# The fourth block's scores and attention moved behind the experts, and a later turn of the first expert's tokens

## The reference

```python
y = xn @ U                                   # 128 -> 32
dist = n[:, None] + n[None, :] - 2 * y @ y.T # n = sum(y*y), per block
attn = softmax(-dist) @ xn                   # 512 x 512 per block

probs = softmax(rms(xn) @ router_w.T)        # 8 experts, the best 2
dispatch = the first 320 tokens of each expert, in order
routed += w * ((silu(xg @ rg[e]) * (xg @ ru[e])) @ rd[e])   # inner size 512
shared = (silu(xn @ sg) * (xn @ su)) @ sd                   # inner size 1024
out = x + attn + shared + routed
```

## Time and profile before

| | us |
|---|---|
| median of 3 runs | 157.55 (156.96 to 157.59) |
| the profiled execution, its own time | 156.88 |
| its span, first to last instruction | 155.4 |
| PE busy | 150.5 |
| DVE busy | 117.4 |
| ACT busy | 103.5 |
| POOL busy | 83.2 |

### The profile page before, as it was taken

The page is one execution under the profiler, slowest core; times in us unless marked ns, Lnnn a source line. Parts: engine busy times, 40 slices in busy tenths (PEclk is TensorE's granted clock), DMA queues, the critical chain, the costliest instruction groups (busy, mean ns, idle before and its releaser), DMA issues.

```text
span 155.4 us, 3117 instructions
## 1 busy us (share of the span) xinstructions
PE 150.5 (97%) x964; PEld 135.1 (87%) x964; DVE 117.4 (76%) x290; ACT 103.5 (67%) x217; POOL 83.2 (54%) x102
## 2 busy tenths in 40 slices
PE   6999999999999999999999999999999999999992
PEld 6878777889999888888888899999999999878991
DVE  3999969899735599998988777786786786546871
ACT  3369999999469397768756569889677466334100
POOL 7653422357777787877400005698988847454000
PEclk9999999999999999999999999999999999999999
DMA  4999999981111117435069300423232011118486
GB/s 128 302 275 111 210 308 343 343 245 54 55 53 51 51 54 218 158 80 172 0 173 259 124 0 2 152 58 98 67 103 72 25 46 34 30 32 291 96 273 186
DMA packets 26638, 20.72 MB, mean 133 GB/s; under 512 B 2333, under 2 KB 22840, under 8 KB 26624
## 3 DMA queue, kind: packets, MB, share of 16 engines
q1 hardware_dynamic: 24544, 17.76, 42.4%
q0 software_dynamic: 1792, 2.65, 5.6%
q10 hardware_dynamic: 288, 0.14, 0.3%
HBM read 12.36 MB, written 7.92 MB: 131 GB/s over the span
## 4 chain that ended last, share of the span: by engine, by line
PE 92%; DVE 2%; DMA 2%; ACT 1%; POOL 1%; issue 1%; DVEq 0%
PE bank L1259 9%; PE bank L1344 9%; PE bank L1179 8%; PE bank L1181 8%; PE bank L1180 8%; PE bank L1290 8%; PE bank L1284 8%; PE bank L1287 8%; PE bank L1400 5%; PE bank L1402 5%; PE bank L1401 5%; PE bank L1416 2%; PE bank L1244 2%; PE bank L1427 2%; DMA acc<-in_L_attn_x_dram 2%; PE bank L1199 1%
## 5 line engine op out<-in xcount | busy, mean ns | idle before, releaser
L673 ACT ACTIVATE silu<-bank 128x512 f32<-128x512 f32 (+1 forms) x64 | 33.3, 520 | 29.5 <-PE bank L1290 28.9
L567 POOL DMA_INDIRECT slots_dram<-row,slot_i x32 | 34.0, 1063 | 10.9 <-issue 9.4
L1010 DVE TENSOR_TENSOR bank<-bank,silu 128x320 f32<-128x320 f32 (+1 forms) x48 | 27.1, 565 | 15.5 <-ACT silu L673 12.6
L586 POOL DMA_INDIRECT routed_dram<-eo,xg x24 | 23.0, 957 | 11.5 <-DVE eo L1050 6.3
L1016 DVE TENSOR_TENSOR hid_lo<-bank,hid_hi 128x320 fp32r<-128x320 f32 (+1 forms) x48 | 26.2, 546 | 0.0
L681 ACT CAST hid_hi<-bank 128x320 fp32r<-128x320 f32 (+1 forms) x48 | 22.9, 477 | 0.0
L574 POOL TENSOR_TENSOR ew_lo<-sw_raw,ew_hi 128x1024 fp32r<-128x1024 f32 x3 | 7.2, 2414 | 19.3 <-ACT ew_hi L697 19.3
L1010 DVE TENSOR_TENSOR hid_s<-bank,silu 128x512 f32<-128x512 f32 x16 | 11.0, 686 | 5.6 <-PE bank L1181 5.2
L1344 PEld LDWEIGHTS bank<-sd,hid_s 128*128 128x128 f32 x128 | 14.8, 192 | 0.3
L1259 PEld LDWEIGHTS bank<-row,probs 128*128 128x128 f32 x128 | 14.8, 191 | 0.2
L1344 PE MATMUL bank<-sd,hid_s 128*128 128x128 f32 x128 | 15.0, 275 | 0.0
(11 more groups left out here) (204 smaller groups left out, 362.6 us busy)
## 6 DMA issues: line engine op xcount, KB each, us to landing
sw_raw<-in_L_ffn_rg_dram SPq DMA_DIRECT2D x8, 256.0 KB, 3.1
sw_raw<-in_L_ffn_ru_dram SPq DMA_DIRECT2D x8, 256.0 KB, 3.6
rd_raw<-in_L_ffn_rd_dram SPq DMA_DIRECT2D x8, 256.0 KB, 3.4
routed_dram<-fill SPq DMA_DIRECT2D x1, 2048.0 KB, 11.7
routed<-routed_dram SPq DMA_DIRECT2D x8, 256.0 KB, 4.1
slots_dram<-fill SPq DMA_DIRECT2D x1, 1300.0 KB, 12.2
xg<-slots_dram SPq DMA_DIRECT2D x8, 130.0 KB, 2.4
row<-row SPq DMA_DIRECT2D x1, 1024.0 KB, 7.7
```

Source lines behind the costliest of these rows:

```text
L567: G.indirect_dma_start(slots_dram, bass.IndirectOffsetOnAxis(slot_i[:, k, t:t + 1], 0), row[:, t, 0:RW], None, bounds_check=E * CAP - 1, o ...
L673: C.activation(silu[:, q % 2, 0:n], gate_bank(q)[:, 0:n], ACT.Silu).then_inc(silu_ready, 1)
L1010: V.tensor_tensor(hid, up[:, 0:n], silu[:, q % 2, 0:n], ALU.mult).then_inc(hid_ready, 1)
```

## The change

The scores and the attention of the fourth block leave the place before block 1. The scores now stand between the gate and up products of the last chunk of all, into other banks; the exponentials come at the end of ACT's program, into memory of the loaded weights; the two halves of attention stand inside `down_end_block`, between the second and the third group of the f32 down products. DVE adds the attention there, and SP's last two stores wait for it. The first expert's tokens are turned behind the last up product of block 2 and not behind its sixth chunk, and the down product that stood at the first expert's first chunk moves one step forward. The second pair of expert down weights gets another place (that of `xnT` of block 0), since the fourth block's `yL` and `yR` stay in use.

```diff
     def down_step(q):
+        if q == at["block", EARLY - 1, CS - 3]:
+            return at["block", EARLY - 1, CS - 1]
         return CLOSE if q == END else min(q + LAG, END + 1)
...
+        rd_hi, rd_lo = [[in_y[:, CS * D:CS * D + CR * D].rearrange("p (c d) -> p c d", c=CR),
+                         in_x[:, 0:CR * D].rearrange("p (c d) -> p c d", c=CR)]
+                        for in_y, in_x in ((yL, xnT_hi), (yR, xnT_lo))]
+        end_probs = sw_raw[:, :, :].rearrange("p s (j i) -> p (s j) i", i=S)
+        def probs_of(b):
+            return end_probs if b == B - 1 else probs[:, b % 2, :, :]
...
+        end_score_b = [bank[7], bank[4], bank[5], bank[6]]
+        end_down_b = [bank[0], bank[1]]
+        end_att_b = [bank[2], bank[3]]
...
             for h in range(2):
+                sp.wait_ge(att_added, 2 * (B - 1) + h + 1)
                 sp.wait_ge(block_added, B + h)
...
-                    if j == 0 and b >= 2:
+                    if j == 0 and b == B - 1:
+                        act.wait_ge(ew_split_pool, E - DVE_WEIGHTS)
+                    elif j == 0 and b >= 2:
                         act.wait_ge(att_done, 2 * (b - 1))
...
             def round_down_weights(e):
                 act.wait_ge(rd_loaded[e % 2], 16 * (e // 2 + 1))
+                if e == 1:
+                    act.wait_ge(chunk_done, CS)
...
             act.wait_ge(sd_loaded, 16)
-            exps(3)
             C.copy(sd_hi, sd[:, :, :]).then_inc(sd_hi_s, 1)
...
-                    elif c == 6:
+                    elif c == 7:
                         slots_hi(0)
...
+            exps(B - 1)
...
-            for b in range(1, B):
+            for b in range(1, B - 1):
                 add_attention(b, 0)
                 add_attention(b, 1)
...
-                    elif c == 6:
+                    elif c == 7:
                         slots_lo(0)
...
             end_block_sum(0)
+            dve.wait_ge(block_added, B)
+            add_attention(B - 1, 0)
+            add_attention(B - 1, 1)
+            dve.wait_ge(att_added, 2 * B)
             end_block_sum(1)
...
+                elif b == B - 1:
+                    pe.wait_ge(eo_ready, E)
+                    pe.wait_ge(hid_ready, len(ORDER) - 2)
+                    pe.wait_ge(xg_ready, E)
+                    pe.wait_ge(out_copied, len(JOBS))
...
             def down_end_block():
                 b = B - 1
-                first, second = turn_b[0], sums_b
-                pe.wait_ge(xg_ready, E)
-                pe.wait_ge(hid_ready, at["block", b, CS - 2])
+                first, second = end_down_b
+                pe.wait_ge(silu_ready, at["block", b, CS - 1])
+                pe.wait_ge(hid_ready, at["block", b, CS - 1])
                 down_tile(first[:, 0:D], 0, range(CS - 2))
-                pe.wait_ge(out_copied, len(JOBS))
                 down_tile(second[:, 0:D], 2, range(CS - 2))
                 pe.wait_ge(hid_ready, at["block", b, CS - 1] + 1)
                 down_tile(first[:, 0:D], 0, range(CS - 2, CS))
                 down_tile(first[:, D:2 * D], 1).then_inc(end_down, 1)
+                attend(b, 0)
+                attend(b, 1)
                 down_tile(second[:, 0:D], 2, range(CS - 2, CS))
                 down_tile(second[:, D:2 * D], 3).then_inc(end_down, 1)
...
             attend(2, 0)
-            scores(3)
             attend(2, 1)
-            attend(3, 0)
-            attend(3, 1)
...
+                    elif q == len(ORDER) - 1:
+                        between = lambda: scores(B - 1)
...
+                if (kind, i, c) == ("block", EARLY - 1, CS - 1):
+                    turn_slots(0)
                 for p in chunks_down(q):
                     down_chunk(p)
...
-                if (kind, i, c) == ("block", EARLY - 1, 5):
-                    turn_slots(0)
-                elif kind == "expert" and c == 0 and i + 1 < E:
+                if kind == "expert" and c == 0 and i + 1 < E:
                     turn_slots(i + 1)
```

More of the change, by code:

```diff
@@ L216, in down_weights_of @@
             if s < 2:
-                return rd_hi[:, s, :, :], rd_lo[:, s, :, :]
+                return rd_hi[s], rd_lo[s]
             return rd_more[:, s - 2, 0, :, :], rd_more[:, s - 2, 1, :, :]
@@ L228, in moe_attention_kernel @@
         assert CS == 2 * TG and B % 2 == 0
-        assert CS * D + 2 * CR * D <= T
+        assert CS * D + CR * D <= (B - 1) * S and CR * D <= S
         sd_hi, sd_lo = [t[:, 0:CS * D].rearrange("p (c d) -> p c d", c=CS) for t in (yL, yR)]
-        rd_hi, rd_lo = [t[:, CS * D:CS * D + 2 * CR * D].rearrange("p (s c d) -> p s c d", s=2, c=CR)
-                        for t in (yL, yR)]
+        rd_hi, rd_lo = [[in_y[:, CS * D:CS * D + CR * D].rearrange("p (c d) -> p c d", c=CR),
[4 more added lines that the diff above has]
+            return end_probs if b == B - 1 else probs[:, b % 2, :, :]
         turned_out = sb("turned_out", [P, S])
@@ L257, in moe_attention_kernel, with score_bank, att_bank @@
         turn_b = [bank[6], bank[7]]
+        end_score_b = [bank[7], bank[4], bank[5], bank[6]]
+        end_down_b = [bank[0], bank[1]]
+        end_att_b = [bank[2], bank[3]]
+        def score_bank(b, j):
+            return end_score_b[j] if b == B - 1 else bank[j]
+        def att_bank(b, h):
+            return end_att_b[h] if b == B - 1 else down_b[h]
         tokens_b = [bank[6], bank[0], bank[3], bank[0]]
@@ L662, in exps @@
                     act.wait_ge(score_done, t + 1)
-                    if j == 0 and b >= 2:
+                    if j == 0 and b == B - 1:
+                        act.wait_ge(ew_split_pool, E - DVE_WEIGHTS)
+                    elif j == 0 and b >= 2:
                         act.wait_ge(att_done, 2 * (b - 1))
-                    C.activation(probs[:, b % 2, j, :], bank[j][:, :], ACT.Exp, scale=2.0
+                    C.activation(probs_of(b)[:, j, :], score_bank(b, j)[:, :], ACT.Exp, scale=2.0
                                  ).then_inc(prob_ready, 1)
@@ L695, in round_weights @@
                     elif e >= 3:
-                        act.wait_ge(att_done, 2 * B)
+                        act.wait_ge(att_done, 2 * (B - 1))
                 C.copy(weights_of(e)[0][:, w, :], ew_raw[:, e % 2, w, :]).then_inc(ew_hi_s, 1)
@@ L994, in add_attention @@
                 dve.wait_ge(att_done, 2 * b + h + 1)
[L995 removed]
+                o = att_bank(b, h)[:, 0:2 * (D + 1)].rearrange("p (r c) -> p r c", r=2)
                 t = TG * b + 2 * h
@@ L1057, in end_block_sum @@
                 a = acc[:, t:t + 2, :].rearrange("p t d -> p (t d)")
-                V.tensor_tensor(a, (turn_b[0], sums_b)[h][:, 0:2 * D], a, ALU.add).then_inc(block_added, 1)
+                V.tensor_tensor(a, end_down_b[h][:, 0:2 * D], a, ALU.add).then_inc(block_added, 1)
             def add_routed(k, g):
@@ L1116, in _ @@
             add_attention(0, 1)
-            for b in range(1, B):
+            for b in range(1, B - 1):
                 add_attention(b, 0)
                 add_attention(b, 1)
-                if b == B - 2:
-                    dve.wait_ge(sd_hi_s, 1)
-                    V.tensor_tensor(sd_lo, sd[:, :, :], sd_hi.bitcast(F32), ALU.subtract).then_inc(sd_split, 1)
+            dve.wait_ge(sd_hi_s, 1)
+            V.tensor_tensor(sd_lo, sd[:, :, :], sd_hi.bitcast(F32), ALU.subtract).then_inc(sd_split, 1)
             for q in range(FIRST, len(ORDER)):
@@ L1241, in scores @@
                         pe.wait_ge(hid_ready, CS)
-                    else:
+                    elif b < B - 1:
                         pe.wait_ge(prob_ready, TG * (b - 1) + j + 1)
-                    M(bank[j][:, :], yL[0:NR.stop, S * b + P * j:S * b + P * j + P],
+                    M(score_bank(b, j)[:, :], yL[0:NR.stop, S * b + P * j:S * b + P * j + P],
                       yR[0:NR.stop, S * b:S * b + S], start=True, stop=True).then_inc(score_done, 1)
@@ L1250, in attend @@
                 pe.wait_ge(prob_ready, TG * (b + 1))
-                if b >= 1:
+                if 1 <= b < B - 1:
                     pe.wait_ge(att_added, 2 * (b - 1) + h + 1)
+                elif b == B - 1:
+                    pe.wait_ge(hid_ready, len(ORDER))
                 elif h == 0:
@@ L1258, in attend @@
                     for j in range(TG):
-                        last = M(down_b[h][:, (D + 1) * (i % 2):(D + 1) * (i % 2 + 1)],
-                                 probs[:, b % 2, j, P * i:P * i + P], xn_ones[:, TG * b + j, :],
+                        last = M(att_bank(b, h)[:, (D + 1) * (i % 2):(D + 1) * (i % 2 + 1)],
+                                 probs_of(b)[:, j, P * i:P * i + P], xn_ones[:, TG * b + j, :],
                                  start=(j == 0), stop=(j == TG - 1))
@@ L1305, in up_chunk @@
                 elif q == FIRST + 2:
-                    pe.wait_ge(att_added, 2 * B - 1)
+                    pe.wait_ge(att_added, 2 * (B - 1) - 1)
                 elif q - 3 in nth_split:
@@ L1395, in down_chunk @@
```

(11 more changed lines are left out.)

## The result

The changed kernel takes 161.31 us (median of 6 runs, 159.76 to 161.54) against 157.43 for the kernel before (6 runs, 156.96 to 157.99): a ratio of 1.0221, 95% interval 1.0171 to 1.0271. It is slower, as forecast, but by 3.9 us where 2.0 over the median were forecast; 161.31 lies outside the range of 157.3 to 160.8.

The account below looks back on a forecast made before the run. PE, busy 97% of the span, was taken as the bound. Front -4.50, end +4.50, token wait +2.7 and split +0.05 gave +2.8 on 156.88: 159.6 us, range 157.3 to 160.8 (forecast's own 159.1 to 160.3).

Parts of the forecast that it names:

- Front and end, net 0.0: Fourth block's scores and attention: 4.50 us leave the front and the same 4.50 us come back at the end.
- cover to spare: At the end: PE has 6.6 us of work while ACT's table load and exponentials take 3.94; 2.7 us spare.
- DVE 0.40 late into block 1: Front pulled forward: DVE enters the second block 0.40 us late; 0 to 0.40 could reach PE, taken as 0.
- The scatters held by DVE's subtracts: POOL's scatters inside two-SBUF-operand subtracts run longer: holds 4.1 us against 2.43 before, so scatters end 1.70 us later.
- the prediction's lock: POOL's scatters beside a full DVE: one held scatter makes the next one held too.
- Rivals 1 and 2: 1: scatters end as before, wait 1.01, 157.9 us, chance 0.20; 2: scatters escape the subtracts, 156.9 us, chance 0.08.
- The wait of 2.7 us: First expert's tokens: PE there at 78.65, turn possible only at 81.36, so PE waits 2.7 us.
- The split chain behind the turn, 0.05: ACT's copy and DVE's subtract before the first expert: about 1.5 us against 1.7 of PE work, cost taken 0.05.
- The sum: All terms together: +2.8 us on the profiled execution's 156.88, giving 159.6 us.
- rival 3: Lock begins a scatter earlier or lasts longer, 2.5 us and over: wait 3.5, 160.4, up to 161 us; chance 0.12.

Follow-up runs that it names:

- free scatters: DVE's weight subtracts read one operand from PSUM, low parts left out: changed kernel 157.85 us; kernel before with only the later turn 157.47 us.
- the turn last: Changed kernel with the turn of the first tokens behind the two down chunks, not ahead of them: 160.78 us, ratio 1.0195.
- block 3's chunks: Changed kernel with the fourth block's first two chunks ahead of the experts, the turn between them, down step as in the kernel before: 158.36 us, ratio 1.0064.
- the kernel with 6.1 us of idle time: Changed kernel with only the moved attention; turn, its split and down step back where they were: 165.82 us, ratio 1.0526.

## Why the prediction was wrong

- **Front and end, net 0.0: right.** Scores, exponentials and attention at the end wait for nothing, cover to spare 2.4 us (2.7 predicted). With free scatters the spans with and without the moved attention have the same median. The sum took the time outside the span to stay at 1.5 us; in the changed kernel it is 1.74 to 1.95, 0.25 or so more, and no run shows why.
- **DVE 0.40 late into block 1, taken as 0: right.** From 47.6 to 78 PE is busy for all 30.40 us.
- **The scatters held by DVE's subtracts: right, shown by taking the hold away.** Predicted holds 4.13 us and the last scatter at 76.50; the profiled execution has 3.3 and 76.04, since DVE's short wait ended the row of held scatters (the prediction's lock) after four. In the runs with the turn last and with block 3's chunks six stand in a row, as laid out, and the last scatter starts at 76.35 and 76.43. The turn was predicted at 81.36 and came at 81.09, 81.22, 81.44 and 81.63 in four kernels. Rivals 1 and 2 fell with that.
- **The wait of 2.7 us: right as an event, a little long.** PE was predicted there at 78.65 and was free at 78.97 (the whole row of this execution began 0.3 later: the first product of block 0 at 8.92 in place of 8.62); the pause was 2.1.
- **The split chain behind the turn, 0.05: right where there is a pause.** With the pause filled and the clock full the first expert's gate follows the last down product without a gap (83.18, 83.41). Where PE comes to the turn without a pause it costs 0.35 us (85.27 for 84.92), since DVE's split then stands behind another one in its queue; the working left that case out.
- **The sum, "-4.50 + 4.50 + 2.7 + 0.05 = +2.8": this step failed.** It let a pause of PE cost its own length and nothing more. Behind the pause the granted clock was 0.50 for over 3 us, and the same instructions took 4.21 us in place of 2.66: 1.55 us that the sum did not have. Only rival 3 named it in half a sentence ("if the pause costs further time"), tied to a longer lock, at 0.6 us (160.4 to 161) and with no row. In the two runs at full clock the sum holds: spans of 158.0 and 158.1 are 2.6 and 2.7 over 155.4. From 159.6 to 161.31 are 1.7 us, and roughly they come to this: 1.55 for the clock, 0.25 outside the span, and 0.55 because the sum stands on an execution of 156.88 where the median was 157.43, less 0.6 for a pause of 2.1 in place of 2.7. A kernel whose every window shows a clock of 1.00 has no row for the price; a bound from both sides would have been the instructions behind the pause at half the pace.

What stays open: why the clock falls in four of six runs of the changed kernel and two of four with the turn last, at the same idle times as far as the times tell. All four runs of the kernel with 6.1 us of idle time had it, and none of the kernels with a single idle time of 1.01 or less (idle times as in the profiled executions). Open as well is what lengthens the time outside the span.

## What to carry to other kernels

Price a new pause of TensorE twice: its length, and the work that stands behind it at half the pace. If the pause can't be avoided, useful or even useless products in it can win back the second part (here 1.2 us), but work taken from behind the pause can open a second one there, as with the turn last. And before pulling PE work forward, look for the slowest supply behind it: here scatters whose pace depends on which instructions of DVE run beside them.

## What the runs showed of the hardware

- A scatter of POOL that starts in the first 0.15 us of a DVE subtract of two SBUF operands (128x512) takes 1.41 to 1.50 us in place of 0.97, and less the later it starts (1.16 us at 0.37); with one operand in PSUM it takes 0.97. Where both engines are full the two fall into step, four scatters in a row in the changed kernel's trace and six in four others.
- After about 2 us without a product the granted clock fell to 0.50, some 0.8 us after the products began again, and stayed there for over 3 us of full work; four of six runs show the lower mean clock (0.989). With 32 small bf16 products in that time and 1.01 us of idle time left it stayed at 1.00.
- Two idle times of 1.02 and 1.09 us, with three small products between them, had the same effect in two of four runs; a single one of 0.46 or 1.01 had none.
